# Vision tower kernel: expert blocks in four interleaved runs with weights fetched only where a slot lacks them, rows scattered to their tokens, and attention values of the four-layer stage on row tiles

## The reference

```python
# L1_ffn_ref: four layers ("T5"), 12 heads of width 64, an expert part in layers 1 and 3
for i in range(L):
    nx = t5_layer_norm(h, ln1[i])
    q = (nx @ attn_q[i]).reshape(b, s, H, DK)
    ...
    attn = jax.nn.softmax(scores, axis=-1)
    ctx = jnp.einsum('bhqk,bkhd->bqhd', attn, v).reshape(b, s, H * DK)
    h = h + ctx @ attn_o[i]
    nx = t5_layer_norm(h, ln2[i])
    y = jax.nn.relu(nx @ ffn_wi[i]) @ ffn_wo[i]
    if i in MOE_LAYERS:      # (1, 3); 8 experts, the best 2 for each token
        y = y + moe_ffn(nx.reshape(-1, d), gate_w[mi], moe_w1[mi], moe_w2[mi]).reshape(b, s, d)
    h = h + y
# moe_ffn and L2_ffn_ref (16 experts, best 2), for each expert e:
h = jax.nn.gelu(jnp.einsum('bld,df->blf', x, W1e) + b1e, approximate=False)   # 192 -> 768
out = jnp.einsum('blf,fd->bld', h, W2e) + b2e                                 # 768 -> 192
y = y + ge[..., None] * out
```

## Time and profile before

| What | Value |
|---|---|
| Runs (three) | 1951.66, 1955.34, 1963.25 us; median 1955.34 us |
| Profiled execution | 1953.65 us, its span 1951.6 us |
| PE busy | 1457.1 us (75%) |
| DVE, ACT, POOL busy | 751.5, 437.1, 359.3 us |
| Mean granted PE clock | 0.851 of full speed |
| DMA | 152.00 MB, 78 GB/s over the span |

### The profile page before, as it was taken

The page is one execution under the profiler, slowest core; times in us unless marked ns, Lnnn a source line. Parts: engine busy times, 40 slices in busy tenths (PEclk is TensorE's granted clock), DMA queues, the critical chain, the costliest instruction groups (busy, mean ns, idle before and its releaser), DMA issues. The chain is left out here.

```text
span 1951.6 us, 26183 instructions
## 1 busy us (share of the span) xinstructions
PE 1457.1 (75%) x9530; PEld 1049.9 (54%) x9530; DVE 751.5 (39%) x1866; ACT 437.1 (22%) x916; POOL 359.3 (18%) x387
## 2 busy tenths in 40 slices
PE   5569649778877996587897599918637995765998
PEld 5355323544364886246536389913427995343666
DVE  3446653533462111346237311144641111474244
ACT  0410423232231111222222211103102331221221
POOL 0000642202113002311103210034221103340000
PEclk8769759998997998788999699958658998876999
DMA  4010210100103685010001338820018984101000
GB/s 110 1 36 3 65 53 0 62 13 0 62 14 111 177 259 155 15 61 14 0 0 63 102 101 258 232 58 3 1 39 227 261 264 147 30 3 49 25 25 16
DMA packets 60678, 152.00 MB, mean 78 GB/s; under 512 B 15960, under 2 KB 36000, under 8 KB 59824
## 3 DMA queue, kind: packets, MB, share of 16 engines
q1 hardware_dynamic: 52256, 133.39, 23.3%
q0 software_dynamic: 8304, 17.02, 2.6%
HBM read 134.26 MB, written 16.12 MB: 77 GB/s over the span
## 5 line engine op out<-in xcount | busy, mean ns | idle before, releaser
L1072 PE MATMUL bank<-t_xgT,t_ew 96*128 96x128 f32 x1104 | 134.4, 279 | 2.8 <-DVE t_xgT L1142 2.8
L1072 PEld LDWEIGHTS bank<-t_xgT,t_ew 96*128 96x128 f32 x1104 | 132.3, 196 | 3.8 <-DVE t_xgT L1142 3.8
L312 PE MATMUL bank<-ident,xn 128*96 128x128 f32 x128 | 28.9, 420 | 105.4 <-DVE xn L291 105.4
L1640 PE MATMUL bank<-xT,wA 128*128 128x512 f32 x192 | 97.3, 630 | 7.7 <-PEq L149 7.7
L1247 PE MATMUL bank<-xT,w 96*128 96x512 f32 x192 | 86.5, 610 | 15.4 <-ACTq L1321 15.4
L1086 PE MATMUL bank<-t_ew,t_hg 128*128 128x192 f32 x552 | 97.0, 326 | 0.0
L1072 PE MATMUL bank<-l_xgT,l_ew 96*128 96x128 f32 x744 | 92.1, 282 | 1.0 <-DVE l_xgT L1145 1.0
L1360 DVE SCALAR_TENSOR_TENSOR h<-bank,cw,h 128x192 f32<-128x192 f32 x128 | 53.5, 418 | 100.3 <-PE bank L1263 83.8
L1072 PEld LDWEIGHTS bank<-l_xgT,l_ew 96*128 96x128 f32 x744 | 90.8, 199 | 1.7 <-DVE l_xgT L1145 1.7
L1702 PE MATMUL bank<-t_ptb,t_v 128*64 128x128 f32 x768 | 55.5, 300 | 45.6 <-DVE t_ptb L568 45.6
L307 PE MATMUL bank<-ident,xn 128*128 128x128 f32 x64 | 26.9, 422 | 83.4 <-DVE xn L289 83.4
(11 more groups left out here) (281 smaller groups left out, 2761.6 us busy)
## 6 DMA issues: line engine op xcount, KB each, us to landing
t_ew<-in_t_moe SPq DMA_DIRECT2D x92, 576.0 KB
l_ew<-in_l_w SPq DMA_DIRECT2D x62, 576.0 KB
wA<-in_t_wqkv SPq DMA_DIRECT2D x5, 1728.0 KB
w<-in_l_w SPq DMA_DIRECT2D x8, 576.0 KB, 5.5
t_xg<-rows_in SPq DMA_DIRECT2D x46, 96.0 KB, 6.1
rows_out<-t_og POOLq DMA_DIRECT2D x46, 96.0 KB, 5.2
patches<-in_patches SPq DMA_DIRECT2D x8, 384.0 KB, 6.8
rows_in<-zero SPq DMA_DIRECT2D x1, 2976.0 KB, 10.8
```

The costliest lines, as they stand in the source:

```text
L312: mm = pe.transpose(k.bank[2 * (t // 4) + c][0:CH, cols], k.xn[:, t, c * CH:(c + 1) * CH], k.ident[:])
L1072: mm = pe.matmul(k.bank[2 + 2 * (b % 2) + m // 4][:, (m % 4) * P:(m % 4 + 1) * P], k.ew1[s][:, c, m * P:(m + 1) * P], k.xgT[b % 2][:, c, : ...
L1640: pe.matmul(k.bank[(i + o) % 8][:], w[:, which, (m + o) * P:(m + o + 1) * P], k.xTs[:, 0, cols], start=True, stop=False)
```

## The change

1. **T5 values on row tiles.** `ptb` now has 32 instead of 128 query columns; one DVE transpose of 128x384 replaces four of 32x384, and POOL clears nothing. `value` multiplies each group of 32 partitions by itself: 48 matmuls per tile of 32 rows by 64 columns with 32 moving columns, in the order head pair, head, row group, each row group into its own bank. Four banks are used for one tile, so there is one set of result banks instead of two: the values of tile t wait for the copies of tile t-1. ACT makes four copies of 128x192 instead of two of 128x384.
2. **Blocks in four interleaved runs.** There are four weight slots; the sorted list is cut in four runs, and slot s works through run s (`sorted_block`). POOL fetches the weights of a block (both matrices and the bias in one row of 2,304 or 2,310 floats per partition) by an indirect DMA. Where the expert is that of the block before in the same run, 2^20 is added to the row numbers; such rows are past the bound and nothing is moved. The instruction is issued all the same, for every block.
3. **Rows scattered home.** The rows carry two more columns, twice the token's number and the expert of its second choice, and the 64 last columns twice (258 floats instead of 192). For each block DVE works out where each row belongs (`dest`), and POOL scatters the result to `rows_out`, which has two rows for each token. At the end SP loads them by 8 plain DMAs; the 16 gathers of POOL are gone. Unused places must hold a marker, so `rows_in` is filled anew before each expert part (by SP, in the T5 and level 2 projection phases) instead of once in the level 1 attention.
4. **128 + 64 split** in the expert blocks: `first` is 6 matmuls over 128 rows, then 6 over 64 rows in alternating halves. Level 2's norm and router use the same split. ACT waits for the whole of `first`.
5. `plan_blocks` has six more small DVE instructions. Four small constants more are loaded at the start.

```diff
@@ -31,7 +31,11 @@
-X_SLOTS, W_SLOTS, O_SLOTS = 3, 3, 3
+X_SLOTS, W_SLOTS, O_SLOTS = 3, 4, 3
+ROW = DIM + REST + 2
+C_TOKEN, C_SECOND = DIM + REST, DIM + REST + 1
+EXPERT = SPLIT + FC * DIM
+SKIP = 2.0 ** 20
...
+def chain_starts(nb):
+
+    lengths = [len(range(s, nb, W_SLOTS)) for s in range(W_SLOTS)]
+    return [sum(lengths[:s]) for s in range(W_SLOTS)]
...
+def sorted_block(i, nb):
+
+    return chain_starts(nb)[i % W_SLOTS] + i // W_SLOTS
...
@@ -515,8 +546,10 @@
+    o_ring = 2 if spread else 1
     def o_banks(t):
-        return k.bank[2 + 2 * (t % 2)], k.bank[3 + 2 * (t % 2)]
+        return (k.bank[2 + 2 * (t % 2)], k.bank[3 + 2 * (t % 2)]) if spread else k.bank[2:6]
...
+                    if t >= o_ring:
+                        pe.wait_ge(k.ctx_copied, t + 1 - o_ring)
                     value(pe, t, ptb[t % 2], o_banks(t)).then_inc(k.pv_done, 1)
...
-                    for j in range(QUADS):
-                        rows = slice(j * QUAD, (j + 1) * QUAD)
-                        ins = dve.transpose(ptb[t % 2][rows, :, rows], pr[t % 3][rows, :, :])
+                    if spread:
+                        for j in range(QUADS):
+                            rows = slice(j * QUAD, (j + 1) * QUAD)
+                            ins = dve.transpose(ptb[t % 2][rows, :, rows], pr[t % 3][rows, :, :])
+                    else:
+                        ins = dve.transpose(ptb[t % 2][:], pr[t % 3][:])
...
@@ -974,13 +1013,32 @@
+    link(dve.tensor_tensor(k.picked[:, 0, :, 0:n_e], k.sel[:, 1, :, 0:n_e],
+                           k.iota[:, 0:n_e].unsqueeze(1).broadcast_to([P, NT, n_e]), ALU.mult))
+    link(dve.tensor_reduce(k.rows[:, :, C_SECOND], k.picked[:, 0, :, 0:n_e], AX_X, ALU.add))
...
-    link(dve.tensor_reduce(k.owner_f[:, 0:nb], passed, AX_X, ALU.add))
-    link(dve.tensor_scalar(k.owner[:, 0:nb], k.owner_f[:, 0:nb], float(n_e - 1), None, ALU.min))
+    mine, last = k.owner[:, 1:nb + 1], k.owner[:, 0:nb]
+    source = k.source_f[:, 0:nb]
+    link(dve.tensor_reduce(mine, passed, AX_X, ALU.add))
+    link(dve.tensor_scalar(mine, mine, float(n_e - 1), None, ALU.min))
+    link(dve.tensor_tensor(k.same[:, 0:nb], mine, last, ALU.is_equal))
+    link(dve.tensor_scalar(source, mine, float(P), part, ALU.mult, ALU.add))
+    link(dve.tensor_tensor(k.same[:, 0:nb], k.same[:, 0:nb], k.cont[0 if n_e == 8 else 1][:], ALU.mult))
+    link(dve.tensor_tensor(k.source[:, 0:nb], source, k.same[:, 0:nb], ALU.add))
...
+def fetch_expert(pool, k, i, nb, weights):
...
+    b = sorted_block(i, nb)
+    pool.indirect_dma_start(k.ew[i % W_SLOTS][:, 0:weights.shape[1]], None, weights,
+                            bass.IndirectOffsetOnAxis(ap=k.source[:, b:b + 1], axis=0),
+                            bounds_check=weights.shape[0] - 1, oob_is_err=False
+                            ).then_inc(k.expert_loaded[i % W_SLOTS], 16)
...
-            for b in range(W_SLOTS if started else 0, nb):
-                s, x = b % W_SLOTS, b % X_SLOTS
-                e = sp.value_load(k.owner[0:1, b:b + 1], min_val=0, max_val=n_e - 1)
...
-                if b >= W_SLOTS:
-                    sp.wait_ge(k.l1_done, 2 * (b - W_SLOTS + 1))
...
+            if send:
+                sp.wait_ge(k.owner_known, 1)
+            for b in range(X_SLOTS if started else 0, nb):
+                x, row = b % X_SLOTS, sorted_block(b, nb) * P
                 if b >= X_SLOTS:
-                    sp.wait_ge(k.rows_turned, b - X_SLOTS + 1)
-                sp.dma_start(k.xg[x][:], k.rows_in[b * P:(b + 1) * P, :]).then_inc(k.x_loaded[x], 16)
-                if b >= W_SLOTS:
-                    sp.wait_ge(k.l2_done, b - W_SLOTS + 1)
-                sp.dma_start(k.ew2[s][:], w2).then_inc(k.w2_loaded[s], 16)
+                    sp.wait_ge(k.rows_copied, b - X_SLOTS + 1)
+                sp.dma_start(k.xg[x][:], k.rows_in[row:row + P, :]).then_inc(k.x_loaded[x], 16)
...
+            for t in range(NT):
+                sp.dma_start(k.gg[:, t, :, :].rearrange("p c d -> p (c d)"),
+                             k.rows_out[2 * t * P:2 * (t + 1) * P, :].rearrange("(p c) d -> p (c d)", c=2)
+                             ).then_inc(k.row_in[t], 16)
...
+            if not started:
+                for b in range(W_SLOTS):
+                    fetch_expert(pool, k, b, nb, weights)
             if send:
                 send_rows(pool, k)
                 pool.sem_inc(k.owner_known, 1)
             for b in range(nb):
+                if b + W_SLOTS < nb:
+                    pool.wait_ge(k.l2_done, b + 1)
+                    fetch_expert(pool, k, b + W_SLOTS, nb, weights)
                 pool.wait_ge(k.evacuated_v, b + 1)
-                pool.dma_start(k.rows_out[b * P:(b + 1) * P, :], k.og[b % O_SLOTS][:]).then_inc(k.back[b % O_SLOTS], 16)
+                pool.indirect_dma_start(k.rows_out, bass.IndirectOffsetOnAxis(ap=k.dest[:, b:b + 1], axis=0),
+                                        k.og[b % O_SLOTS][:], None, bounds_check=2 * TOK - 1, oob_is_err=False
+                                        ).then_inc(k.back[b % O_SLOTS], 16)
...
-            for t in range(NT):
-                for c in range(2):
-                    pool.indirect_dma_start(k.gg[:, t, c, :], None, k.rows_out[0:nb * P, :],
-                                            bass.IndirectOffsetOnAxis(ap=k.place_i[:, c, t:t + 1], axis=0)
-                                            ).then_inc(k.row_in[t], 16)
...
-                    mm = pe.transpose(k.bank[b % 2][0:CH, c * P:(c + 1) * P],
-                                      k.xg[b % X_SLOTS][:, c * CH:(c + 1) * CH], k.ident[:])
+                    mm = pe.transpose(k.bank[b % 2][:, c * P:(c + 1) * P],
+                                      k.xg[b % X_SLOTS][:, c * P:(c + 1) * P], k.ident[:])
                 mm.then_inc(k.rows_turned, 1)
 
-                    for c in range(2):
-                        mm = pe.matmul(k.bank[2 + 2 * (b % 2) + m // 4][:, (m % 4) * P:(m % 4 + 1) * P],
-                                       k.ew1[s][:, c, m * P:(m + 1) * P], k.xgT[b % 2][:, c, :],
-                                       start=(c == 0), stop=(c == 1))
-                    if m in (3, FC - 1):
+                    pe.matmul(hidden(b, m % 2)[:, m // 2 * P:(m // 2 + 1) * P], w[:, m * P:(m + 1) * P],
+                              k.xgT[b % 2][:, 0, :], start=(m < 2), stop=False)
+                for m in range(FC):
+                    half = halves[m % 2]
+                    mm = pe.matmul(hidden(b, m % 2)[:, m // 2 * P:(m // 2 + 1) * P],
+                                   w[half, FF + m // 2 * P:FF + (m // 2 + 1) * P], k.xgT[b % 2][half, 1, :],
+                                   start=False, stop=(m >= FC - 2))
+                    if m >= FC - 2:
                         mm.then_inc(k.l1_done, 1)
...
+                    for o in range(2):
+                        ins = act.activation(k.hg[b % 2][:, o:FC:2, :],
+                                             hidden(b, o)[:, 0:FC // 2 * P].rearrange("p (m q) -> p m q", q=P), func)
                 ins.then_inc(k.hid_step, 1)
...
+                    if fills(b, X_SLOTS) > 0:
+                        dve.wait_ge(k.x_loaded[b % X_SLOTS], 16 * fills(b, X_SLOTS))
+                    dve.scalar_tensor_tensor(k.dest[:, b:b + 1], x[:, C_SECOND:ROW], k.owner[:, own:own + 1],
+                                             x[:, C_TOKEN:C_SECOND], ALU.is_equal, ALU.add)
...
-                for b in range(W_SLOTS):
-                    w1, w2, _ = send(sp.value_load(k.owner[0:1, b:b + 1], min_val=0, max_val=7))
-                    sp.dma_start(k.ew1[b][:], w1).then_inc(k.w1_loaded[b], 16)
-                    sp.dma_start(k.ew2[b][:], w2).then_inc(k.w2_loaded[b], 16)
                 sp.wait_ge(k.owner_known, 1)
...
+                for i in range(X_SLOTS):
+                    b = sorted_block(i, blocks_for(8))
+                    sp.dma_start(k.xg[i][:], k.rows_in[b * P:(b + 1) * P, :]).then_inc(k.x_loaded[i], 16)
...
+                for i in range(W_SLOTS):
+                    fetch_expert(pool, k, i, blocks_for(8), send)
                 send_rows(pool, k)
                 pool.sem_inc(k.owner_known, 1)
...
@@ -1699,26 +1752,33 @@
-                mm = pe.matmul(banks[m // 3][64 * o:64 * o + 64, (m % 3) * P:(m % 3 + 1) * P],
-                               v[:, t, (2 * m + o) * 64:(2 * m + o + 1) * 64], pt[:, 2 * m + o, :],
-                               start=True, stop=True)
+                for j in range(QUADS):
+                    rows = slice(j * QUAD, (j + 1) * QUAD)
+                    mm = pe.matmul(banks[j][64 * o:64 * o + 64, m * QUAD:(m + 1) * QUAD],
+                                   v[rows, t, (2 * m + o) * 64:(2 * m + o + 1) * 64], pt[rows, 2 * m + o, :],
+                                   start=True, stop=True)
...
-        return [(qT[:, 3 * i:3 * i + 3, t * P:(t + 1) * P], banks[i][:, 0:3 * P].rearrange("p (m q) -> p m q", q=P))
-                for i in range(2)]
```

(2 more changed lines are left out.)

229 lines of the change are left out of this document (117 added, 112 removed).

## The result

The changed kernel took 1852.29 us in the median of four runs (1847.33 to 1857.8), the kernel before in the same comparison 1953.5: a ratio of 0.9474, 95% interval 0.9428 to 0.952. The profiled execution took 1847.33 us, its span is 1845.5. The forecast was 1834, the range 1803 to 1885.

The account below looks back on a forecast made before the run. The T5 attention was taken as bound by a DVE and POOL loop, expert blocks by PE with waits for rows. Gains 40 + 52 + 35 - 1 - 4.5 - 0.5 = 121 us gave about 1834; 8-in-10 range 1803 to 1885.

Parts of the forecast that it names:

- Transposes, and the loop of DVE and POOL: T5 attention: one transpose of 0.58 us replaces four of 2.32; the DVE and POOL loop shrinks to 3.49 us a tile.
- The value step: T5 attention: 48 short value matmuls take 1.1 us start to start, 0.9 plus 0.2 for a switch; range 0.55 to 3.5.
- The rival in which they don't overlap: T5 attention: 96 value records take 1.76 to 3.5 us; at 2.6 the program takes 1881 us; chance 0.16.
- PE has 8 values, 8 projections and 6 scores: 8.8 + 17.2 + 5.3: T5 attention after the first transposes: 31.3 us of PE work, 1.0 of waits; gains 10 us a layer, 40 in four.
- Expert blocks: T5 and level 2 expert parts: a block every 4.5 us without waits for rows, 71 intervals x 0.735 = 52 us gained.
- a period that stays: Expert blocks: halves don't pair up or DMAs collide, a block still takes 5.2 us, the program 1885; chance 0.11.
- POOL as the limit: Expert blocks: a fetch's cost grows with its bytes to 11.5 us, POOL needs 12.8 a block, far above 2400; chance 0.05.
- the first reason given for the vanished waits: Expert blocks: with at most half the bytes of weights loaded, PE's waits for rows were expected to go.
- the second, rows alone in SP's queue: Expert blocks: with rows alone in SP's queue, PE's waits for rows were expected to go.
- End: After the last expert block: scatter, SP's loads and adds finish at 778.6 instead of 790.25; 11.6 us each, 35 in three.
- Start of level 2 and planning: Level 2's fetches ahead of sends lose 1 us (0 to 6); six more DVE steps lose 4.5 over three plannings.
- the forecast's own range of 1808 to 1862: Whole program as summed, chance 0.66: from values 0.55 with period 4.3 to values 1.5 with period 4.7.

Follow-up runs that it names:

- shift96: Changed kernel with 24 needless score matmuls (96 instructions) after the third tile's scores of each T5 attention: 1851.54 us.
- fetch_all: Changed kernel with every block fetching its weights, also where the slot already holds them: 1860.4 us.
- l2_first: Changed kernel in which POOL at level 2 fetches only block 0's weights ahead of the sends, those of blocks 1 to 3 behind them: 1858.41 us.

## Why the forecast came out as it did

*Transposes, and the loop of DVE and POOL: right.* One of 0.58 a tile, and PE is the limit in the middle of a phase.

*The value step: right in itself.* 1.10 us start to start, 96 records 11.5 ns apart. The rival in which they don't overlap (1.76 to 3.5 us) is out. The Trainium skill (TensorE: Matmul & The Clock Gate, "Wait — 56ns, not 53.3ns?") says that matmuls never start less than about 25 ns apart, which makes an estimated 2.4 us of them; the trace disagrees, with 1.10.

*"PE has 8 values, 8 projections and 6 scores: 8.8 + 17.2 + 5.3": this step failed.* The sum took PE's steps at full clock and, as idle time, 1.0 us at the start. It did not ask whether 312 instructions a tile reach PE in time. The four phases were forecast at 39.3 us from first scores to last add (521.92 to 561.2) and took 45.8 in the mean, 6.5 more. The traces say where, from the first value step to PE's last matmul of a phase:

| Mean of four phases, us | Forecast | Measured |
|---|---|---|
| PE waits for instructions | 0 | 4.55 |
| PE waits for other engines | 1.0 | 0.50 |
| PE works | 31.3 | 34.05 |

So 4.05 of the 6.5 are waits and 2.75 work; the first value step and the last add came 0.3 earlier than counted. (The other 2.0 of the 20.2 us of stops lie ahead of the first value step.) The work is longer where the granted clock is 1.2 instead of 2.4 GHz. In each of the four phases that is a stretch of 10.2 us; in this layer it begins 7.3 us after the first scores, as the first values start and after PE has stood idle for 2.88. A projection takes 3.8 us in it and 2.2 outside (the first row is a stretch by engine as above, its granted clock 0.52):

```profile
515.90:526.60 10.70, 8.91 (x252) 8.18 (x252) 4.54 (x10) 2.92 (x10) 3.24 (x4) 0.52 0.19 76
522.88 3.84 PE L586 MATMUL bank<-wo,t_qT 128*128 128x192 f32 x12
```

In the same phase before, the stretch was 6.8 us long, PE was idle in half of it, and the mean granted clock of the phase was 0.93 instead of 0.89. With the steps of a regular tile (1.10, 2.15, 0.81), and the five scores that remain after the first three tiles, not six, the work would be 30.1. The difference, nearly 4 us a phase, goes with the lower level. The kernel before already paid about 2 of it in three of its four phases. That the stops lengthen the slow stretch was not tried. So the term is 16.8, not 40. The signs were there: the queue of instructions had six packets in a phase of 49.7 us, and the change nearly doubles a tile's instructions while the tile gets shorter.

The Trainium skill (Runtime: NRT & Kernel Launch, "Instruction fetch mechanics") says that each engine's instructions are refilled in blocks of 16 KiB, 256 instructions, and that the cost of crossing a block is mostly hidden. The trace agrees with the size (256, 256, 254 records between stops), and not with the second half where records are 6 to 8 ns apart (192 in 1.10 us, 96 in 0.81): there a block's end costs up to 2.6 us, and once 4.68 in `shift96`.

*Expert blocks: right.* 51.2 against 52; period 4.53 against 4.5, `first` 2.30 against 2.35 and waits gone. The rivals of a period that stays and of POOL as the limit are out: a fetch occupies POOL for 1.04 us whether it has 1.18 MB to move (`fetch_all`) or nothing, a send for 0.97. The fetches that moved weights, 19 and 18, are fewer than the 22 and 19 expected. Halved bytes, the first reason given for the vanished waits, are less than half of it, as `fetch_all` shows; the second, rows alone in SP's queue, is what the rest goes with.

*End: right,* 35.4 against 35: the first add comes 5.5 us after the last copy where 6.7 were summed, and the adds wait once, 0.8. This is read from the two traces; no run changes the end alone.

*Start of level 2 and planning: right in size,* -3.9 against -3, as the difference of two: the first turn comes 8.2 us later, and the first result follows it after 11.9 instead of 16.2. `l2_first` shows that the first turn follows POOL's issue, and not the weights. In T5 the first turns come 2.0 and 0.5 later than before, but the first results 1.6 later and 1.5 earlier; within what the clock changes there, the planning's loss of 3 can't be told.

*Not forecast:* 6.7 us in stretches that the change hardly touches, 7.4 of them before the first T5 attention. There the mean clock up to 350 us was 0.80 instead of 0.77, and the twelve other profiles of changed kernels reach this point at 349.8 to 356.4, in the mean 353.1; whether part of it is real stays open (the filling of `rows_in` moved out of this stretch, and no run undid that). With it the miss of 23 us in the attention became one of 15 between the two profiles (106.1 instead of 121), and of 18 between the forecast and the median. That the whole is this near is in part luck, and so is that it lies in the forecast's own range of 1808 to 1862: its slow end stands for value steps of 1.5 and blocks 4.7 apart, and neither happened (1.10 and 4.53).

## What to carry to other kernels

When a change replaces few long instructions by many short ones, count instructions as well as work: here an engine got 256 per 3.2 us at best, and stretches that used them up nearly as fast stopped at some of the 256ths for up to 2.6 us. Long matmuls put between the short ones gave part of it back, 6 to 8 us of 20; fewer and larger instructions only do where the engine behind them is not loaded more. And where loads are late, look at what stands ahead of them in their queue as well as at the bytes.
